# A transformer layer's MLP: from half batch by half batch with plain products to layer by layer with Strassen's seven products

## The chip, the cores and the metric

One NeuronCore of one Trainium2 chip. The metric is the device time of one execution in microseconds (us), the median of three runs. Engines: PE (TensorE), DVE (VectorE), ACT (ScalarE), POOL (GpSimd), SP (SyncE, which issues most loads and stores), and 16 DMA engines that move the data.

## The reference, cut to what matters

```python
# B, T, C = 8, 512, 512; x: (8, 512, 512); hidden sizes 1024, 1024, 512
h = _layernorm(x, axis=-1) * (1 + ca) + sa
x = x + ga * _L0_attn_ref(h, L0_attn_W_attn, L0_attn_W_proj)
h = _layernorm(x, axis=-1) * (1 + cb) + sb
# _L0_ffn_ref:
x1 = relu(einsum('bpd,hd->bph', h,  W1) + b1)   # 512 -> 1024
x2 = relu(einsum('bpd,hd->bph', x1, W2) + b2)   # 1024 -> 1024
out = einsum('bpd,od->bpo', x2, W3) + b3        # 1024 -> 512
x = x + gb * out
```

ca, sa, ga, cb, sb, gb are modulation vectors per batch. Everything is f32.

## The kernel before, in words

Each f32 product is made of three matmuls. An operand is split into a high part (its value rounded to fp32r) and a low part (the rest), and the high-high, low-high and high-low products are summed in PSUM (`TERMS`). So each operand costs a cast, mostly on ACT, and a subtraction, mostly on DVE.

The program has two parts. `attention` (the first 45% of the time) computes everything up to the attention output per batch and leaves it in DRAM as `attn_dram`. It isn't touched. `mlp` then does the rest. The diff replaces it whole.

`mlp` before works on half a batch (256 tokens, `CH`) at a time, sixteen in all, in a loop over the batches, with the first and last written out. All weights are loaded and split once at the start (`strips_hi` L1086 on ACT, `strips_lo` L1180 on DVE) and stay in SBUF. For a half batch PE does, in this order (`chunk` in the tensor block):

- layer 1 (`hidden`, L1268): 8 blocks of 128 features, 4 x 3 matmuls each, weights stationary, 256 tokens moving;
- turning the attention rows of the next half batch (L1230);
- layer 2 (L1268): 8 blocks of 8 x 3 matmuls, and after two of them the projection of the next half batch (`project`, L1249, 24 matmuls of 512 columns);
- turning the normalised rows of the next half batch (L1239);
- layer 3 (`last_layer`, L1249): 2 blocks of 128 tokens, 8 x 3 matmuls each, data stationary, 512 output columns moving.

ACT applies bias and ReLU to each block of features (L1080) and modulates the turned rows (L1072). DVE casts and subtracts to get the two parts (L1132, L1134), adds the gated attention output to the residual, takes the row statistics and normalises (L1142 to L1158), and finishes the output (L1170 to L1174). POOL only raises the variance to the power -0.5 (L1047). Activations never leave SBUF. The residual `res_tiles` is loaded from x, changed in place and stored from there. The order on every engine is written out by hand, and semaphores count what is done. An engine takes its instructions strictly in that order.

## Time and profile before

| what | us |
|---|---|
| median of three runs (1613.67 to 1619.86) | 1615.04 |
| the profiled execution | 1619.41 |
| its span, first to last instruction | 1617.6 |
| PE busy | 1540.7 (95%) |
| DVE busy | 938.1 (58%) |
| ACT busy | 637.5 (39%) |
| POOL busy | 441.5 (27%) |

The span is what the trace covers. The execution's own time has 1.8 us around it. Line numbers (L1268) are those of the kernel before. Matmuls overlap, so the time that one takes from start to end (0.283 us for 256 columns) is more than the distance from one to the next.

### The profile page before, as it was taken

What the parts mean: (1) busy time and instruction counts of PE and PEld (TensorE: products, weight loads), DVE (VectorE), ACT (ScalarE), POOL (GpSimd) and SP (SyncE); (2) the same over time, 40 slices, a digit from 0 to 9 for tenths busy, and PEclk for the clock granted to TensorE, in tenths of its full rate; (3) what the DMA queues carried; (4) which work ended last, traced back from release to release, by engine and by line L of the source; (5) the groups of instructions that cost most, each with busy time, mean ns of one, the idle gap of its engine ahead of it and who ended that gap; (6) DMA issues with size and microseconds to landing.
All of it is one profiled execution on the core that took longest, in us unless ns stands there. A gap on an engine that the chain in (4) does not pass through costs nothing.

```text
span 1617.6 us, 31407 instructions
## 1 busy us (share of the span) xinstructions
PE 1540.7 (95%) x12112; PEld 1369.6 (85%) x12112; DVE 938.1 (58%) x2199; ACT 637.5 (39%) x1280; POOL 441.5 (27%) x459
## 2 busy tenths in 40 slices
PE   7899999999999999966899999999999999999998
PEld 6678788878888878855899999999999999999998
DVE  4477877787778777646644444444544444444442
ACT  2166666666666666654312121212121212121221
POOL 2156666666666666660000000000000000000000
PEclk9799999999999999987999999999999999999999
DMA  6534343434343433316201001110111011100100
GB/s 215 151 80 126 87 125 87 126 86 126 87 119 93 119 93 93 93 30 223 94 34 47 27 20 48 46 30 31 34 47 46 2 47 46 40 21 34 46 14 14
DMA packets 80546, 118.33 MB, mean 73 GB/s; under 512 B 10632, under 2 KB 31112, under 8 KB 80400
## 3 DMA queue, kind: packets, MB, share of 16 engines
q1 hardware_dynamic: 72416, 105.19, 24.1%
q10 hardware_dynamic: 7984, 11.03, 1.9%
q8 instruction: 111, 1.82, 0.5%
q14 instruction: 35, 0.29, 0.1%
HBM read 48.52 MB, written 16.81 MB: 40 GB/s over the span
## 4 chain that ended last, share of the span: by engine, by line
PE 52%; DVE 1%; DMA 1%; issue 0%; SPq 0%; ACT 0%; POOL 0%; DVEq 0%; POOLq 0%
PE feature L1268 34%; PE token L1249 17%; PE feature L1239 1%; PE token L1230 1%; DVE w L1180 1%; DMA b_rows<-b 0%; DMA w_ring<-wproj_t 0%; DVE y L1134 0%; SPq L1010 0%; DVE y L1132 0%; ACT w L1086 0%; DVE attn_tiles L1158 0%; POOL mlp_rstd L1047 0%; DVE gated L1170 0%; DVE res_tiles L1145 0%
## 5 line engine op out<-in xcount | busy, mean ns | idle before, releaser
L1268 PE MATMUL feature<-y,w 128*128 128x256 f32 x3072 | 376.2, 283 | 6.5 <-DVE w L1180 6.5
L1268 PEld LDWEIGHTS feature<-y,w 128*128 128x128 f32 x3072 | 372.9, 189 | 8.0 <-DVE w L1180 6.7
L1080 ACT ACTIVATE mlp_full<-feature,b_cols 128x256 f32<-128x256 f32 x256 | 120.1, 474 | 649.5 <-PE feature L1268 561.2
L433 POOL TENSOR_TENSOR prob_lo<-prob,prob_hi 128x512 f16<-128x512 f32 x256 | 297.1, 1165 | 143.4 <-ACT prob L537 142.9
L1132 DVE CAST y<-mlp_full 128x256 fp32r<-128x256 f32 x256 | 75.0, 293 | 304.1 <-ACT mlp_full L1080 303.7
L530 ACT ACTIVATE prob_hi<-key_score 128x512 f16<-128x512 f32 x320 | 191.0, 597 | 134.7 <-PE key_score L828 132.3
L1047 POOL TENSOR_TENSOR mlp_rstd<-mlp_var_eps,mlp_minus_half 128x2 f32<-128x2 f32 x16 | 11.1, 696 | 802.9 <-DVE mlp_var_eps L1153 802.9
L739 PE MATMUL lin<-h_parts,wqkv 128*128 128x512 f32 x768 | 219.5, 410 | 1.1 <-DVE h_parts L582 1.1
L1268 PEld LDWEIGHTS feature<-turned,w 128*128 128x128 f32 x1536 | 188.2, 190 | 8.2 <-DVE w L1180 3.8
L1268 PE MATMUL feature<-turned,w 128*128 128x256 f32 x1536 | 189.4, 283 | 5.8 <-DVE turned L1134 3.4
L537 ACT ACTIVATE prob<-key_score 128x512 f32<-128x512 f32 x320 | 190.5, 595 | 0.0
L701 DVE TENSOR_REDUCE row_max<-score 128x1 f32<-128x512 f32 (+2 forms) x384 | 180.4, 498 | 13.8 <-PE score L815 13.1
L1249 PE MATMUL token<-w,y 128*128 128x512 f32 x768 | 183.5, 398 | 0.0
L1249 PEld LDWEIGHTS token<-w,y 128*128 128x128 f32 x768 | 143.4, 188 | 33.7
L739 PEld LDWEIGHTS lin<-h_parts,wqkv 128*128 128x128 f32 x768 | 144.0, 196 | 30.0 <-DVE h_parts L582 2.5
L815 PE MATMUL score<-stack 96*128 96x512 f32 (+3 forms) x512 | 156.2, 367 | 0.0
L828 PE MATMUL key_score<-stack 98*128 98x512 f32 (+3 forms) x512 | 144.7, 345 | 0.0
L848 PEld LDWEIGHTS o_bank<-v_parts,prob_hi 128*128 128x128 f16 x1280 | 100.1, 99 | 28.9 <-issue 25.5
L848 PE MATMUL o_bank<-v_parts,prob_hi 128*128 128x97 bf16 x1280 | 117.3, 212 | 5.2 <-POOL prob_lo L433 2.5
L848 PE MATMUL o_bank<-v_parts,prob_lo 128*128 128x65 bf16 x1280 | 114.4, 196 | 0.0
L1134 DVE TENSOR_TENSOR y<-mlp_full,y 128x256 fp32r<-128x256 f32 x256 | 108.9, 425 | 8.7
L749 PE MATMUL lin<-wqkv,h_parts 128*128 128x256 f32 x768 | 108.9, 284 | 0.0
(93 smaller groups left out, 1927.6 us busy)
## 6 DMA issues: line engine op xcount, KB each, us to landing
stack<-qk_parts SPq DMA_DIRECT2D x384, 128.0 KB, 2.4
x_tiles<-x SPq DMA_DIRECT2D x32, 256.0 KB, 3.8
attn_dram<-o_rows SPq DMA_DIRECT2D x32, 256.0 KB, 2.3
attn_tiles<-attn_dram SPq DMA_DIRECT2D x16, 512.0 KB, 5.0
res_tiles<-x SPq DMA_DIRECT2D x16, 512.0 KB, 3.5
out<-res_tiles ACTq DMA_DIRECT2D x16, 512.0 KB, 3.0
w_ring<-w_t SPq DMA_DIRECT2D x12, 512.0 KB, 5.6
wmod_sb<-wmod SPq DMA_DIRECT2D x4, 1024.0 KB, 6.3
```

Of the source, the lines that this page charges most:

```text
L433: nc.gpsimd.tensor_tensor(prob_lo[:, key[1] % 2, u, :], prob[:, u, :], prob_hi[:, key[1] % 2, u, :], ALU.subtract).then_inc(lo_pool, 1)
L530: nc.scalar.activation(prob_hi[:, q % 2, u, :], bank[:], ACT.Exp, scale=SOFTMAX_SCALE, bias=P_SHIFT)
L537: nc.scalar.activation(prob[:, u, :], bank[:], ACT.Exp, scale=SOFTMAX_SCALE, bias=P_SHIFT)\
L701: last = nc.vector.reduce_max(row_max[:, p % 2, hh, t:t + 1], bank[:, col:col + P * (t + 1)], AX.X)
L739: mm = nc.tensor.matmul(lin_bank_of((QK, f))[:], wqkv[:, wl, c, at:at + P], h[:, hl, c, :], start=(c == 0 and k == 0), stop=(c == NC_ - 1 ...
L749: mm = nc.tensor.matmul(lin_bank_of((V, g, t))[:, 0:C // 2], h[:, hl, c, t * P:(t + 1) * P], wqkv[:, wl, c, at:at + C // 2], start=(c == 0 ...
L815: mm = nc.tensor.matmul(bank[:, col:col + n], rows[:, 0, t * P:(t + 1) * P], rows[:, 1, 0:n], start=False, stop=True, skip_group_check=True)
L828: mm = nc.tensor.matmul(bank[:, col:col + n], rows[:, 1, t * P:(t + 1) * P], rows[:, 0, t * P:T], start=False, stop=True, skip_group_check ...
L848: mm = nc.tensor.matmul(o_bank[:, i * VW + low:(i + 1) * VW], part[:, p % 2, u, at:at + P], v[:, j, head, low:VW], start=(j == 0 and part ...
L1080: nc.scalar.activation(full[:, f % 2, :], fbank[f % 4][:, 0:CH], ACT.Relu, bias=bias[:, f:f + 1])\
L1249: mm = nc.tensor.matmul(bank[:], data[:, dl, c, t * P:(t + 1) * P], weights[:, wl, c, :], start=(c == 0 and i == 0), stop=(c == chunks - 1 ...
L1268: mm = nc.tensor.matmul(fbank[f % 4][:, 0:CH], weights[:, wl, c, f * P:(f + 1) * P], data[:, dl, c, :], start=(c == 0 and i == 0), stop=(c ...
```

## The change

The MLP now runs layer by layer over all batches: layer 1 for batches 0 to 7 (`EXPAND`), then layer 2 (`MIDDLE`), then layer 3 (`CONTRACT`), 24 chunks of one batch each, without a loop. Each chunk is the product of a weight matrix and a data matrix, both cut in 2 x 2 blocks, by Winograd's form of Strassen's scheme. Seven half-size products `product(n, s)`, s = 0 to 6, take the place of eight. Each still is three matmuls per term, now all with 256 columns.

- The sums of data blocks that four of the operands need are made by POOL (`sums`, 4 per chunk), those of the weights by POOL and DVE, once per layer (`w1_sums`, `w2_sum`, `w3_sums`).
- Operand s of chunk n is cast by ACT (`hi`) and subtracted by DVE (`lo`) into a ring of three buffers. Its buffer is free when product s - 3 is done.
- The seven results go to three pairs of PSUM banks (`SUMS`). ACT copies the first (`first_product`), DVE adds the others up to the four result blocks (`second_sum`, `third_sum`, `make_c22`, `make_c21`, `make_c12`), and C11 is accumulated by PE.
- ACT applies bias and ReLU in place (`relu`, 16 instructions a chunk), and SP stores the four blocks to `y_dram` (64 stores of 512 KB). Two layers load them back block by block (`load_block`, 64 loads).
- The residual after attention, with b3 times the gate already added by POOL, goes to `x2_dram` and is loaded again in the last layer, where DVE multiplies the blocks by the gate (`gate`) and POOL adds them (`add_gated`).
- Only weights of the layer at work are in SBUF. The middle layer's are loaded and split during the chunks 5 to 8, the last layer's in chunk 15.
- Projection, turning, statistics and normalising of the following batches are hung into the products of the first layer by the table `AUX_AT`: (s, m) gives the place, the number behind the kind says how many batches ahead. They share two PSUM banks.

```diff
-CH = 256
-CT = CH // P
-HALVES = T // CH
...
+HB = T // 2
+EXPAND, MIDDLE, CONTRACT = range(3)
+CHUNKS = 3 * B
+STEPS = 7
+K_TILES, M_TILES, BANKS = (2, 4, 4), (4, 4, 2), (2, 2, 1)
...
+SUMS = ("a", "b", "e", "a", "b", "e", "b")
+FRESH = (True, True, True, False, True, True, False)
...
+AUX_AT = {(0, 3): [(PROJ, 1, 2)], (1, 3): [(PROJ, 1, 3)],
+          (2, 1): [(TURNED, 2, 0)], (2, 3): [(TURNED, 2, 1)], (3, 1): [(TURNED, 2, 2)], (3, 3): [(TURNED, 2, 3)],
+          (5, 1): [(ROWS, 1, 0)], (5, 3): [(ROWS, 1, 1)], (6, 1): [(ROWS, 1, 2)],
+          (6, 3): [(ROWS, 1, 3), (PROJ, 2, 0), (PROJ, 2, 1)]}
...
+            def load_block(n, i):
+
+                if n > B:
+                    m = n - 1
+                    if i < 2:
+                        sp.wait_ge(op_sum, sum_no(m, 3) + 1)
+                        sp.wait_ge(op_ready, op_no(m, 0) + 1)
+                    elif i == 2:
+                        sp.wait_ge(op_ready, op_no(m, 3) + 1)
+                    else:
+                        sp.wait_ge(op_ready, op_no(m, 6 if layer(m) < CONTRACT else 5) + 1)
+                elif i >= 2:
+                    sp.wait_ge(op_sum, sum_no(B - 1, 3) + 1)
+                    sp.wait_ge(op_ready, op_no(B - 1, 6) + 1)
+                sp.wait_ge(y_out[i], 16 * (n - B + 1))
+                sp.dma_start(blk[i][:], y_view(n - B, i).rearrange("p (c n) -> p c n", n=HB)).then_inc(blk_in[i], 16)
+
+            def store_block(n, i):
+                sp.wait_ge(relu_done, relu_no(n, i, 3) + 1)
...
+            def load_x2(k):
+                if k >= 2:
+                    for half in range(2):
+                        sp.wait_ge(out_done[half], 16 * (k - 1))
+                sp.wait_ge(x2_out[k % 2], 16 * (k // 2 + 1))
+                sp.dma_start(x2t[:, k % 2], rows_of(x2_dram, k)).then_inc(x2_in[k % 2], 16)
+
...
+            def contract(n):
+                k = n - CONTRACT * B
+                if k:
+                    store_out(k - 1, 0)
+                else:
+                    store_block(n - 1, C12)
+                if k and k + 1 < B:
+                    load_gate(k + 1)
+                if k + 1 < B:
+                    load_block(n + 1, 0)
+                    load_block(n + 1, 1)
+                if k and k + 1 < B:
+                    load_x2(k + 1)
+                if k + 1 < B:
+                    load_block(n + 1, 2)
+                    load_block(n + 1, 3)
+                store_out(k, 1)
+
...
+            def sums(n):
...
+                block_wait(pool, n, 1)
+                block_wait(pool, n, 3 if contract_op else 0)
+                if n:
+                    pool.wait_ge(op_ready, op_no(n - 1, 4) + 1)
+                if contract_op:
+                    nc.gpsimd.tensor_tensor(t1, b[1], b[3], ALU.add).then_inc(op_sum, 1)
+                else:
+                    nc.gpsimd.tensor_tensor(t1, b[1], b[0], ALU.subtract).then_inc(op_sum, 1)
+
+                block_wait(pool, n, 0 if contract_op else 3)
+                ring_wait(pool, n, 1)
+                pool.wait_ge(op_sum, sum_no(n, 0) + 1)
+                if contract_op:
+                    nc.gpsimd.tensor_tensor(low[0], t1, b[0], ALU.subtract).then_inc(op_sum, 1)
+                else:
+                    nc.gpsimd.tensor_tensor(low[0], b[3], t1, ALU.subtract).then_inc(op_sum, 1)
+
+                block_wait(pool, n, 2)
+                if n:
+                    last = max(s for s, i in TEMP_OPS[layer(n - 1)].items() if i == 1)
+                    pool.wait_ge(op_ready, op_no(n - 1, last) + 1)
+                pool.wait_ge(op_sum, sum_no(n, 1) + 1)
+                if contract_op:
+                    nc.gpsimd.tensor_tensor(t4, b[2], low[0], ALU.subtract).then_inc(op_sum, 1)
+                else:
+                    nc.gpsimd.tensor_tensor(t4, low[0], b[2], ALU.subtract).then_inc(op_sum, 1)
+
+                ring_wait(pool, n, 2)
+                if contract_op:
+                    nc.gpsimd.tensor_tensor(low[1], b[0], b[1], ALU.subtract).then_inc(op_sum, 1)
+                else:
+                    nc.gpsimd.tensor_tensor(low[1], b[3], b[1], ALU.subtract).then_inc(op_sum, 1)
+
...
+            def modulate(k, c):
+                no = AUX_NO[(ROWS, k, c)]
+                act.wait_ge(aux_done, no + 1)
+                if k:
+                    act.wait_ge(op_sum, sum_no(k - 1, 3) + 1)
+                    act.wait_ge(op_ready, op_no(k - 1, 0 if c < 2 else 6) + 1)
+                nc.scalar.activation(h2[:, c, :], aux_bank[no % 2][:], ACT.Identity,
+                                     scale=mod_cols[:, 1, NC_ + c, k:k + 1], bias=mod_cols[:, 1, c, k:k + 1])\
+                    .then_inc(rows_act, 1)
...
+            def relu(n, i):
+                bias = (b1_cols, b2_cols)[layer(n)]
+                for m in range(4):
+                    here = made[i][:, m // 2, m % 2 * HB:m % 2 * HB + HB]
+                    src = here
+                    if i == C11:
+                        if m % 2 == 0:
+                            act.wait_ge(prod_done, done_no(n, 3, m // 2) + 1)
+                        if m == 0 and n:
+                            act.wait_ge(y_out[C11], 16 * n)
+                        src = acc["a"][m // 2][:, m % 2 * HB:m % 2 * HB + HB]
+                    elif m % 2 == 0:
+                        act.wait_ge(post_done, post_no(n, {C22: Y22, C21: Y21, C12: Y12}[i], m // 2) + 1)
+                    f = 4 * BLOCKS[i][0] + m
+                    nc.scalar.activation(here, src, ACT.Relu, bias=bias[:, f:f + 1]).then_inc(relu_done, 1)
...
+            def expand(n):
+                k = n
+                last = k == B - 1
+                hi(n, 2)
+                if n:
+                    relu(n - 1, C12)
+                first_product(n)
+                hi(n, 3)
+                hi(n, 4)
+                for c in (0, 1):
+                    if k + 2 < B:
+                        turned_hi(k + 2, c)
+                hi(n, 5)
+                for c in (2, 3):
+                    if k + 2 < B:
+                        turned_hi(k + 2, c)
+                if last:
+                    w2_hi(0)
+                relu(n, C11)
+                hi(n, 6)
+                for c in (0, 1):
+                    if k + 1 < B:
+                        modulate(k + 1, c)
+                if last:
+                    w2_hi(1)
+                relu(n, C22)
+                hi(n + 1, 0)
+                relu(n, C21)
+                for c in (2, 3):
+                    if k + 1 < B:
+                        modulate(k + 1, c)
+                hi(n + 1, 1)
+
+            def middle(n):
...
+            def second_sum(n):
+                for half in halves(n):
+                    dve.wait_ge(prod_done, done_no(n, 1, half) + 1)
+                    dve.wait_ge(p1_done, p1_no(n, half) + 1)
+                    if half == 0:
+                        buffer_free(n, C12)
+                    nc.vector.tensor_tensor(part(u2, n, half), bank_of(n, 1, half)[:], part(p1, n, half), ALU.add)\
+                        .then_inc(post_done, 1)
...
+            def middle(n):
+                make_c12(n - 1)
+                lo(n, 1)
+                lo(n, 2)
+                if n == B:
+                    w2_lo(4)
+                lo(n, 3)
+                second_sum(n)
+                if n == B:
+                    w2_lo(2)
+                lo(n, 4)
+                third_sum(n)
+                if n == B:
+                    w2_lo(3)
+                lo(n, 5)
+                if n == B:
+                    w2_lo(6)
+                lo(n, 6)
+                if n == B:
+                    w2_lo(5)
...
+            def product(n, s):
+                where, tiles = layer(n), K_TILES[layer(n)]
+                if n % B == 0:
+                    pe.wait_ge(w_ready, W_NO[(where, s, 1) if where == MIDDLE else (where, s)] + 1)
+                pe.wait_ge(op_ready, op_no(n, s) + 1)
+                data = op(n, s)
+                for m in range(M_TILES[where]):
+                    if m % 2 == 0:
+                        sum_free(n, s, m // 2)
+                    again = not FRESH[s] or m % 2 == 1
+                    dst = bank_of(n, s, m // 2)[:, m % 2 * HB:m % 2 * HB + HB]
+                    for c in range(tiles):
+                        for i, (wl, dl) in enumerate(TERMS):
+                            begin = FRESH[s] and m % 2 == 0 and c == 0 and i == 0
+                            end = c == tiles - 1 and i == 2
+                            cols = slice(m * P, (m + 1) * P)
+                            if where == CONTRACT:
+                                mm = nc.tensor.matmul(dst, data[:, dl, c, cols], w3[s][:, wl, c, :],
+                                                      start=begin, stop=end, skip_group_check=again)
+                            else:
+                                w = (w1, w2)[where][s]
+                                mm = nc.tensor.matmul(dst, w[:, wl, c, cols], data[:, dl, c, :], start=begin, stop=end,
+                                                      skip_group_check=again)
+                    if m % 2:
+                        mm.then_inc(prod_done, 1)
+                    if where == EXPAND:
+                        for item in aux_at(n, s, m):
+                            aux(item)
+
```

In full length it is 1,500 lines. The functions of the same name per engine (`expand`, `middle`, `contract`) set the order on each engine; the DMA stores and loads all stand in SP's queue.

Three places of the new order, on the engines that wait or are waited for there. The first is ACT, in a chunk before (one half batch; `mlp_full` is the result of bias and ReLU, `turned` the operand):

```order
L1113 DMA out<-res_tiles 128x2x512 [waits out_ready]
L1080 ACTIVATE mlp_full<-feature,b_cols 128x256 [waits f_split,f_done] x8
L1065 CAST turned<-token 128x256 [waits t_done] x4
L1080 ACTIVATE mlp_full<-feature,b_cols 128x256 [waits f_split,f_done] x8
L1072 ACTIVATE mlp_full<-feature,mlp_mod_now 128x256 [waits mlp_mod_ready,f_split,f_done]
L1072 ACTIVATE mlp_full<-feature,mlp_mod_now 128x256 [waits f_split,f_done] x3
L1113 DMA out<-res_tiles 128x2x512 [waits out_ready]
```

and in a chunk of the expanding layer now, from the modulation of the first two blocks of normalised rows to the cast of the next chunk's operands (`p_c` holds C22, `u_c` C21 and then C12, `h` the modulated rows, `op` an operand):

```order
L1438 ACTIVATE h<-aux,mod_cols 128x512 [waits op_ready,op_sum,aux_done] x2
L1482 ACTIVATE p_c<-p_c,b_cols 128x256 [waits post_done]
L1482 ACTIVATE p_c<-p_c,b_cols 128x256
L1482 ACTIVATE p_c<-p_c,b_cols 128x256 [waits post_done]
L1482 ACTIVATE p_c<-p_c,b_cols 128x256
L1448 CAST op<-h 128x512 [waits prod_done,rows_act]
L1482 ACTIVATE u_c<-u_c,b_cols 128x256 [waits post_done]
L1482 ACTIVATE u_c<-u_c,b_cols 128x256
L1482 ACTIVATE u_c<-u_c,b_cols 128x256 [waits post_done]
L1482 ACTIVATE u_c<-u_c,b_cols 128x256
L1438 ACTIVATE h<-aux,mod_cols 128x512 [waits op_ready,op_sum,aux_done] x2
L1456 CAST op<-op_whole 128x512 [waits op_sum] x2
```

The modulation of the last two blocks (L1438, second place) now stands behind the ReLUs of C22 and C21 and the cast of the next chunk's operand 0.

The second is DVE, at the split of the second layer's weights. Before, in the first half batch (`w` are weights, `y` the split data):

```order
L1132 CAST y<-mlp_full 128x256 [waits f_act]
L1134 TENSOR_TENSOR y<-mlp_full,y 128x256 [waits f_hi]
L1180 TENSOR_TENSOR w<-w_ring,w 128x1024 [waits mlp_w_hi]
L1132 CAST y<-mlp_full 128x256 [waits f_act]
L1134 TENSOR_TENSOR y<-mlp_full,y 128x256 [waits f_hi]
L1180 TENSOR_TENSOR w<-w_ring,w 128x1024 [waits mlp_w_hi]
L1180 TENSOR_TENSOR w<-w_ring,w 128x512 [waits mlp_w_hi] x8
```

and now, in the first chunk of the middle layer (L1751 splits weights, L1663 operands, L1680 and L1689 are `second_sum` and `third_sum`, with `sum_b` and `sum_e` PSUM banks):

```order
L1663 TENSOR_TENSOR op<-blk,op 128x1024 [waits op_hi]
L1680 TENSOR_TENSOR u_c<-sum_b,p_c 128x512 [waits y_out1,p1_done,prod_done]
L1680 TENSOR_TENSOR u_c<-sum_b,p_c 128x512 [waits p1_done,prod_done]
L1751 TENSOR_TENSOR w_2<-w_2_whole,w_2 128x1024 [waits mlp_w_hi] x2
L1663 TENSOR_TENSOR op<-op_sum,op 128x1024 [waits op_hi]
L1689 TENSOR_TENSOR u_c<-sum_e,u_c 128x512 [waits y_out2,post_done,prod_done]
L1689 TENSOR_TENSOR u_c<-sum_e,u_c 128x512 [waits post_done,prod_done]
L1751 TENSOR_TENSOR w_3<-w_3_whole,w_3 128x1024 [waits mlp_w_hi] x2
```

The splits were next to each other, ahead of layer 2. Now each stands behind a sum that waits for a product of the same chunk.

The third is SP. Before, the loads of one chunk in the loop:

```order
L998 DMA attn_tiles<-attn_dram 128x2x512
L58 ISA [waits out_done0]
L1001 DMA res_tiles<-x 128x2x512 [waits out_done0]
L58 ISA [waits out_done0]
L993 ISA [waits t_taken]
L993 DMA gate_attn<-gate_dram 128x512
L1035 ISA
L993 ISA [waits out_ready]
L993 DMA gate_mlp<-gate_dram 128x512
```

and now of a chunk of the contracting layer (`x_tiles` are the residual's, `blk` the four data blocks):

```order
L1235 DMA out<-x_tiles 128x2x512 [waits add_done] x2
L1223 DMA gate_mlp<-gate_dram 128x512 [waits g_done]
L1131 DMA blk<-y_dram 128x1024 [waits y_out0,op_ready,op_sum]
L1131 DMA blk<-y_dram 128x1024 [waits y_out1,op_ready,op_sum]
L1230 DMA x_tiles<-x_dram 128x4x512 [waits x2_out0,out_done1,out_done0]
L1131 DMA blk<-y_dram 128x1024 [waits y_out2,op_ready]
L1131 DMA blk<-y_dram 128x1024 [waits y_out3,op_ready]
L1235 DMA out<-x_tiles 128x2x512 [waits add_done] x2
```

The loads of blocks 2 and 3 for the next chunk stand behind the residual's load, which waits for both stores of the output before.

## Rows read from the trace of the kernel before

**Rows 1.** Page: the span, busy time by engine, the chain by line

```profile
span 1617.6 us, 31407 instructions
...
PE 1540.7 (95%) x12112; PEld 1369.6 (85%) x12112; DVE 938.1 (58%) x2199; ACT 637.5 (39%) x1280; POOL 441.5 (27%) x459
...
PE feature L1268 34%; PE token L1249 17%; PE feature L1239 1%; PE token L1230 1%; DVE w L1180 1%; DMA b_rows<-b 0%; DMA w_ring<-wproj_t 0%; DVE y L1134 0%; SPq L1010 0%; DVE y L1132 0%; ACT w L1086 0%; DVE attn_tiles L1158 0%; POOL mlp_rstd L1047 0%; DVE gated L1170 0%; DVE res_tiles L1145 0%
```

**Rows 2.** Stretches of five half batches: us, busy of each engine, PEclk, DMA share, GB/s

```profile
core 0: us, PE busy (x) PEld busy (x) DVE busy (x) ACT busy (x) POOL busy (x), PEclk, DMA share, GB/s
859.22:912.48 53.26, 53.26 (x377) 49.83 (x377) 25.19 (x62) 10.71 (x24) 0.70 (x1) 1.00 0.10 36
...
sum 267.42, PE 266.61 PEld 249.25 DVE 126.10 ACT 53.62 POOL 3.48; mean PE 53.32 PEld 49.85 DVE 25.22 ACT 10.72 POOL 0.70
```

**Rows 3.** Chain in order of time: start, duration, what

```profile
894.20 17.28 PE feature L1268 x144
912.48 11.23 PE token L1249 x48
...
1600.88 11.24 PE token L1249 x48
```

**Rows 4.** SP's queue in order of time, first load of the MLP

```profile
726.46 0.39 SPq L998 DMA_DIRECT2D attn_tiles<-attn_dram  x1
```

**Rows 5.** ACT by form, MLP; two ReLUs in a row; ACT by form, attention

```profile
L1080 ACT ACTIVATE mlp_full<-feature,b_cols 128x256 f32<-128x256 f32 x256 | 120.1, 474 | 649.5 <-PE feature L1268 561.2 <-issue 60.8 <-DVE res_tiles L1174 23.1
L1086 ACT CAST w<-w_ring 128x1024 fp32r<-128x1024 f32 x12 | 12.6, 1049 | 4.7 <-DMA w_ring<-w_t 4.6
...
926.63 0.91 ACT L1080 ACTIVATE mlp_full<-feature,b_cols 128x256 f32<-128x256 f32 x2 [11.75 <-PE feature L1268]
...
L537 ACT ACTIVATE prob<-key_score 128x512 f32<-128x512 f32 x314 | 186.9, 595 | 0.0
L472 ACT ACTIVATE full<-lin,mod_now 128x512 f32<-128x512 f32 x32 | 25.0, 781 | 18.0 <-PE lin L729 9.9 <-POOL h_parts L407 8.0
```

**Rows 6.** DVE by form, MLP

```profile
L1142 DVE TENSOR_TENSOR gated<-token,gate_attn 128x512 f32<-128x512 f32 x32 | 22.1, 691 | 32.3 <-PE token L1249 32.3
L1180 DVE TENSOR_TENSOR w<-w_ring,w 128x1024 fp32r<-128x1024 f32 x12 | 14.4, 1217 | 0.1
```

**Rows 7.** POOL by form, attention

```profile
L433 POOL TENSOR_TENSOR prob_lo<-prob,prob_hi 128x512 f16<-128x512 f32 x251 | 291.3, 1165 | 141.6 <-ACT prob L537 141.3
L407 POOL TENSOR_TENSOR h_parts<-full,h_parts 128x512 fp32r<-128x512 f32 x32 | 40.6, 1278 | 30.3 <-DVE h_parts L582 30.3
L444 POOL TENSOR_TENSOR o_rows<-o_sum,o_rcp 128x256 f32<-128x256 f32 x61 | 37.5, 615 | 0.0
```

**Rows 8.** Loads and stores of the MLP; stretches with full queues

```profile
attn_tiles<-attn_dram SPq DMA_DIRECT2D x16, 512.0 KB, 5.0
out<-res_tiles ACTq DMA_DIRECT2D x16, 512.0 KB, 3.0
...
730.00:735.00 5.00, 1.97 (x8) 1.57 (x8) 2.24 (x4) 2.70 (x6) 0.00 (x0) 0.50 0.95 324
735.00:740.00 5.00, 4.03 (x10) 3.19 (x11) 1.82 (x5) 2.95 (x6) 0.00 (x0) 0.50 0.99 389
```

**Rows 9.** Stretches around PE's wait for the second layer's weights

```profile
765.00:770.00 5.00, 2.94 (x26) 2.70 (x24) 4.90 (x10) 3.16 (x5) 0.00 (x0) 1.00 0.83 256
770.00:775.00 5.00, 0.60 (x3) 0.60 (x4) 4.93 (x9) 4.06 (x6) 0.00 (x0) 0.59 0.94 303
775.00:780.00 5.00, 5.00 (x33) 5.00 (x33) 3.77 (x6) 2.60 (x5) 0.00 (x0) 0.73 0.79 260
```

**Rows 10.** DVE by form, attention, two tensors of SBUF

```profile
L707 DVE TENSOR_TENSOR prob_lo<-prob,prob_hi 128x512 f16<-128x512 f32 x63 | 46.3, 735 | 22.3 <-ACT prob L537 22.3
L617 DVE TENSOR_TENSOR wqkv<-wqkv_raw,wqkv 128x1024 fp32r<-128x1024 f32 x6 | 8.3, 1407 | 0.7 <-ACT wqkv L506 0.6
```

More of the change, by code:

```diff
@@ new lines, in ring_wait, with temp_view, bank_of, halves @@
+    def ring_wait(engine, n, s):
+        if op_no(n, s) >= 3:
+            before = divmod(op_no(n, s) - 3, STEPS)
+            engine.wait_ge(prod_done, done_no(*before, BANKS[layer(before[0])] - 1) + 1)
+    def temp_view(n, i):
+        return temp[i][:, 0:K_TILES[layer(n)], :]
+    def bank_of(n, s, half):
+        return acc[SUMS[s]][half if layer(n) < CONTRACT else n % 2]
+    def halves(n):
+        return range(BANKS[layer(n)])
+    def part(tile, n, half):
+        return tile[:, half if layer(n) < CONTRACT else n % 2, :]
@@ new lines, in _, with aux_free, turn_attention @@
+            for k in range(B):
+                expand(k)
+            for k in range(B):
+                middle(B + k)
+            for k in range(B):
+                contract(2 * B + k)
+            make_c12(CHUNKS - 1)
+            gate(CHUNKS - 1, C12)
+        @whole.tensor
+        def _(pe):
+            def aux_free(item):
+                no = AUX_NO[item]
+                if no < 2:
+                    return
+                kind, k, i = AUX[no - 2]
+                taken = {TURNED: att_lo, PROJ: proj_taken, ROWS: rows_act}[kind]
+                pe.wait_ge(taken, 4 * k + i + 1)
+            def turn_attention(k, c):
+                bank = aux_bank[AUX_NO[(TURNED, k, c)] % 2]
@@ L1234, in turn_rows @@
             def turn_rows(k, c):
+                bank = aux_bank[AUX_NO[(ROWS, k, c)] % 2]
                 if c == 0:
[L1236 to L1251 removed]
@@ L1307 @@
+            for item in AUX_FIRST:
+                aux(item)
+            for n in range(CHUNKS):
+                for s in range(STEPS):
+                    product(n, s)
 def kernel(L0_attn_x, L0_attn_W_attn, L0_attn_W_proj, L0_ffn_W1, L0_ffn_b1, L0_ffn_W2, L0_ffn_b2, L0_ffn_W3,
```

1048 lines of the change are left out of this document (723 added, 325 removed).

## The prediction

> **What bounds the kernel now.** The page comes first. TensorE (PE) is busy 95% of the span, and two lines of the MLP alone, L1268 and L1249, hold half of the chain that ended last [rows 1]. The table of stretches then says whether that is a steady bound: over five consecutive half batches PE is busy 266.61 of 267.42 us at a granted clock of 1.00 (2.4 GHz), while DVE needs 126.10, ACT 53.62 and POOL 3.48 [rows 2]. So a half batch lasts 53.5 us, all of it PE, and every matmul taken away shortens it until something else arrives late. The chain prices a matmul better than its listed latency: 144 with 256 columns take 17.28 us, 0.120 each, and 48 with 512 columns 11.23 us, 0.234 each [rows 3].
>
> The MLP starts with the first load at 726.46 [rows 4] and ends with its last matmul at 1600.88 + 11.24 = 1612.1 [rows 3]: 885.7 us. Sixteen half batches are 855.7. The other 30 are the start: loads, weight splitting, PE at half clock.
>
> **Term 1, matmuls: -87.5 us.** Per batch the three layers are now 576 matmuls of 256 columns and 96 of 512: 69.1 + 22.5 = 91.6 us. Seven half-size products of 24, 48 and 24 matmuls are 672 of 256 columns: 80.6. That saves 10.9, times 8 is 87.5. The listing confirms 5,376. Projection and turns stay, 107.0 - 91.6 = 15.4 us a batch. Note that the third layer gains less than an eighth: 168 x 0.120 = 20.2 against 22.5, since 256 columns cost 0.120, more than half of 0.234.
>
> What is added lies on the other engines. Per batch in the middle layer: DVE 7 x 1.22 + 10 x 0.69 = 15.4 us [rows 6], ACT 7 x 1.05 + 2 x 0.6 + 16 x 0.47 = 16.1 [rows 5], POOL 4 x 2.27 = 9.1, all under 40.3 us of PE. POOL's 2.27 for 1,024 elements is the line through 0.615 for 256 and 1.165 for 512; the row that writes fp32r gives 1.278 for 512, so 2.5 is the upper bound. I take the first, since the new sums write plain f32 as the 256 row does [rows 7]. Going through DVE's and ACT's queue in the middle layer, every operand is ready more than 2 us before its product. I cost that layer at no wait.
>
> **Term 2, the start: -7.** Weights of the middle layer are no longer needed here, but attention rows, projection weights and x come in 1 MB pieces. By the rates of [rows 8], the projection weights land at about 734.5. Two casts of 1.05, four of 0.6 and the last split bring PE's first projection to 739.8; four of them, the first at half clock, end at 752.4; gating, add, statistics and normalising 756.8; four turns and modulations 761; operand 0 at 762.5; turning batch 1 through two banks 766.5; its two projections 772. PE has then done 23.1 us of work that counts in the steady sum, so 772 - 726.5 - 23.1 = about 23 is lost, where it was 30. Bounds -15 and +3.
>
> **Term 3, a wait in the expanding layer: +21.** A chunk is 20.2 + 15.4 = 35.6 us of PE. Its last item but one is projection of the batch after next, which takes the bank of the third turn and so waits until ACT has modulated it. In ACT's order that stands behind a long queue. From the end of the second turn of rows: modulate 0.78, four ReLUs 1.8 (two take 0.91), cast 0.6 [rows 5], DVE's split of operand 0 0.69, first half of C21 0.69 [rows 6], four ReLUs 1.8, modulate 0.78, hand-overs 0.3: 7.4 us. PE meanwhile has one product, 2.9, and two turns, 1.0. That leaves 3.5 us, in the six chunks that have such a projection: 21. If ReLUs ran at the pace of plain casts it were 14; with a DVE slowed as below, and a hand-over more, 33.
>
> **Term 4, expanding to middle layer: +20.** Now the 1,024 x 1,024 weights' sums and splits stand among DVE's work. In chunk 6 two pairs of sums (2.3 each) go before C22 and C21; through ACT's ReLUs, the modulation and two POOL sums, product 1 of chunk 7 is ready 6.8 us late. Chunk 7 has 20.2 us of PE and about as much of DVE, so nothing is regained: middle products 0 and 1 are 0.3 and 1.2 late. Then the splits of weights 2 and 3 each stand behind the DVE sum that waits for the product just ended: 1.3 + 2.3 = 3.6 us [rows 6] before the next can start, 1.7 more for weight 2, whose DVE queue is late already, and 2.6 for weight 5. 6.8 + 0.3 + 1.2 + 5.3 + 3.6 + 2.6 = 20. Bounds 12 and 30: with sums and splits 16% quicker or slower and one wait less or more.
>
> **Term 5, contracting layer: +40.** PE needs 20.2 us a chunk. There is a loop that needs more. Call A the moment POOL has added the last gated block. SP then stores the half output; behind it in SP's queue stand the gate, blocks 0 and 1, the residual's load (which waits until that store has landed, 3.0 [rows 8], so A + 3.4), and only then blocks 2 and 3. Gate, residual and four blocks are 3.4 MB; at 370 GB/s, between the two full stretches of 324 and 389 [rows 8], 9.2 us, from A + 3.3 to A + 12.5. POOL's first sum needs block 3. Four sums of 2.27 and four adds of 1.165 later [rows 7] comes the next A: 12.5 + 9.1 + 4.7 = 26.3 us. The bound is then no engine but this loop. The change of layer delays the first loads (C12's ReLU behind weight casts), so POOL's second sum ends 23.2 us into chunk 16, the next at 49.4, five periods later 180.7; two sums, cast, split and five products: 202 against 161.3. That is 40. With 2.5 us a sum and 14 us of loads it is 57; with blocks landing at A + 10 it is 25.
>
> The Trainium skill, DMA: Bandwidth & Descriptors (Where 436 GB/s comes from), says that between HBM and SBUF the HBM side binds at about 358 GB/s a core. This trace disagrees, with 389 in a stretch [rows 8]. By the page's figure the loop would be 0.3 us longer, 2 us in all (an estimate from that page).
>
> **Term 6, clock: +4.** After a gap of some 6 us the granted clock was 0.59 in the next stretch and 0.73 in that after, then 1.00 again [rows 9]: about 3.3 us at 1.2 GHz, 1.6 lost. Term 4 has two or three such gaps. In the contracting layer PE has 5 us to spare. Gaps of 3.5 us I take as free (bound: 1.6 each, 10).
>
> **Sum.** -87.5 - 7 + 21 + 20 + 40 + 4 = -9.5. The tail (sum, gate, add, store) stays as long. Against the profiled execution, 1619.4 us (span 1617.6), that gives 1609.9; this execution lay 4.4 above the median of the runs shown, 1615.0, so 1605.5. All low bounds together give -52, all high ones +49.
>
> **Rivals.**
> *The loads keep up.* If blocks 2 and 3 land before POOL needs them, the contracting layer is held only by POOL's three sums, cast and split, 9.2 us where PE's three products give 8.6. Term 5 falls from 40 to about 8: 1573.5. For it: the 512 KB loads of the MLP landed in 5.0 us in the median, and 3.0 for stores [rows 8], with DMA mostly idle. Against it: SP's order, in which the loads are not issued earlier whatever they take.
>
> *POOL slows beside DVE: slower than before.* Place: POOL's sums and adds in the loop of term 5. Beside a busy POOL, DVE's two-input subtraction from SBUF took 0.735 and 1.407 us where the same shapes take 0.69 and 1.22 in the MLP [rows 6, 10]. POOL's rows were all taken in the attention part, where DVE reads mostly PSUM; now DVE's seven splits a chunk read two tensors of SBUF. Six sums' worth of POOL work lies in each of six periods, 40 in all with the last. To be 0.5% slower than before needs 17.5 us more, 0.44 a sum: it decides from 2.71 us. At 2.85 (23 us), and DVE 16% slower in terms 3 and 4 (4), +27: 1632.5. Beside this stands the Trainium skill, GPSIMD Engine Reference (8. Key points): POOL shares its SBUF interfaces with DVE, with contention when DVE has two SBUF inputs. By that rule the trace agrees for DVE; for POOL no row shows it.
>
> *The clock falls at each gap of the expanding layer.* +10: 1615.5, no change. For it: [rows 9]. Against: the stretch in which that gap began still shows 1.00.
>
> *The change does not do what it says:* the listing excludes it.
>
> **How the numbers follow.** Forecast 0.5, loads keep up 0.15, POOL slows 0.25, clock 0.1. A run can tell 0.5%, 8 us, from no change. The forecast's own spread is about 20 us around 1605.5: 0.3 faster, 0.1 same, 0.1 slower. The first rival is faster, the second slower but for 0.05, the third mostly same. Faster 0.49, same 0.2, slower 0.31. The range, 1570 to 1642, takes in both rivals and leaves out 2 in 10: an unseen wait above, the low bounds together below.
>
> **What would show it.** Middle chunks of 40.3 us with PE busy throughout; L1990 and L1994 at 0.120 a matmul (right for term 1). PE's L1934 waiting for ACT's L1438 six times, 3.5 each (term 3). PE waiting for DVE's weight splits L1751 near the first middle chunk (term 4). Contracting chunks at 26 us, POOL's L1310 waiting for the block's load, sums of 2.27 (term 5). Contracting chunks of 21 would prove the first rival, sums over 2.7 the second. I am wrong altogether if the middle layer waits too.

## The result, and the profile after

The changed kernel takes 1682.6 us (median of 4 runs, 1680.8 to 1687.1), the kernel before 1615.4 beside it: a ratio of 1.042, 95% interval 1.0385 to 1.0447. That is slower by 4%, and outside the range of the prediction. The profiled execution spans 1679.0.

The page, with the lines that answer to [rows 1]:

```profile
span 1679.0 us, 30398 instructions
...
PE 1479.9 (88%) x12112; PEld 1340.3 (80%) x12112; DVE 1056.3 (63%) x1795; ACT 789.9 (47%) x1430; POOL 830.2 (49%) x661
...
PE 21%; POOL 5%; DMA 5%; DVE 2%; issue 2%; ACT 1%; SPq 0%; POOLq 0%; DVEq 0%; ACTq 0%
```

PE is busy for 61 us less and its share of the span falls from 95% to 88%. (The matmuls taken away are 87.5 us; the difference is mostly matmuls that took longer, as told below. The chain in the last line is followed over little more than a third of the span.) What a steady stretch looks like now, in the middle layer and in the contracting one (windows, as in [rows 2]):

```profile
1140.00:1380.00 240.00, 240.00 (x2002) 240.00 (x2001) 100.84 (x101) 89.15 (x150) 55.84 (x25) 1.00 0.30 109
...
1500.00:1530.00 30.00, 20.74 (x159) 20.53 (x159) 17.55 (x16) 7.72 (x8) 15.42 (x8) 0.84 0.43 150
1530.00:1560.00 30.00, 20.61 (x163) 20.41 (x162) 17.72 (x16) 7.72 (x8) 15.64 (x9) 0.84 0.44 149
```

The middle layer is PE alone. In the contracting layer no engine is busy for more than 70% of the time, and PE waits. The waits of PE over the MLP:

```profile
PE sum_b L1990 <- DVE op L1663: 69.2, 8, 10.3
PE aux L1934 <- ACT h L1438: 18.3, 6, 3.1
PE aux L1944 <- DVE norm_tiles L1651: 14.4, 1, 14.4
...
PE sum_b L1994 <- DVE op L1663: 7.3, 1, 7.3
...
PE sum_b L1994 <- issue: 5.3, 1, 5.3
PE sum_e L1994 <- DVE w L1751: 5.0, 2, 3.1
PE sum_a L1994 <- DVE w L1751: 3.1, 1, 3.1
```

From the timeline of PE and SP the MLP, first load to last matmul, divides as below (us). The last column is the number that the prediction implies.

| stretch | after | predicted |
|---|---|---|
| first load to product 0 of chunk 0 | 60.2 | 46 |
| chunks 0 to 5 (expanding) | 240.8 | 235 |
| chunks 6 to 8 | 119.3 | 112 |
| chunks 9 to 15 (middle) | 284.3 | 282 |
| chunks 16 to 23 (contracting) | 247.8 | 201 |
| sum | 952.4 | 876 |

Before, it was 885.7. So 67 us were lost there, 76 more than forecast; the attention part was 5.9 us shorter in this execution (first load at 720.55 against [rows 4]), which has nothing to do with the change: in the kernels below, which leave it alone too, that load stands between 722 and 726.

PE's time in each stretch can be split into its waits (every idle time of more than 0.1 us) and the rest, and the rest compared with the same matmuls at their steady pace (an expanding chunk without a wait takes 34.8 us in the kernels below, not 35.6):

| stretch | waits of PE | the rest | the rest at the steady pace |
|---|---|---|---|
| chunks 0 to 5 | 20.0 | 220.8 | 209 |
| chunks 6 to 8 | 22.7 | 96.6 | 88 |
| chunks 9 to 15 | 1.8 | 282.5 | 282.2 |
| chunks 16 to 23 | 70.1 | 177.7 | 161.3 |

The slower matmuls stand behind the waits, and the granted clock shows why. First the 5 us behind a wait of 3.05 us in the expanding layer, then chunks 0 to 5 together:

```profile
815.00:820.00 5.00, 4.98 (x12) 3.93 (x13) 0.00 (x0) 1.55 (x3) 3.79 (x3) 0.50 0.26 105
785.00:1021.00 236.00, 217.23 (x1462) 201.23 (x1463) 138.03 (x230) 98.35 (x195) 116.13 (x85) 0.94 0.43 151
```

**The loop of the contracting layer**, in the timeline of SP and of POOL, for one period. SP:

```profile
1564.06 1.64 SPq L1235 DMA_DIRECT2D out<-x_tiles  x2
1565.74 0.50 SPq L1223 DMA_DIRECT2D gate_mlp<-gate_dram  x1
1566.35 1.35 SPq L1131 DMA_DIRECT2D blk<-y_dram  x2
1568.52 0.37 SPq L1230 DMA_DIRECT2D x_tiles<-x_dram  x1
1568.98 1.27 SPq L1131 DMA_DIRECT2D blk<-y_dram  x2
```

POOL:

```profile
1561.76 3.53 POOL L1385 TENSOR_TENSOR x_tiles<-x_tiles,u_c 128x512 f32<-128x512 f32 x2
1579.88 2.34 POOL L1310 TENSOR_TENSOR op_sum<-blk 128x1024 f32<-128x1024 f32 x1 [14.59 <-DMA blk<-y_dram]
...
1589.49 2.26 POOL L1385 TENSOR_TENSOR x_tiles<-x_tiles,c 128x512 f32<-128x512 f32 x1
1591.71 2.26 POOL L1385 TENSOR_TENSOR x_tiles<-x_tiles,p_c 128x512 f32<-128x512 f32 x1
1593.93 2.25 POOL L1385 TENSOR_TENSOR x_tiles<-x_tiles,u_c 128x512 f32<-128x512 f32 x1
```

The last add ends at 1565.3. The residual's load is issued 3.2 us later, as forecast, and the last two blocks behind it. The first sum starts 14.6 us after that add (forecast 12.5), when block 3 has landed, four sums take 9.6 with their hand-overs (9.1), and four adds about 8 (4.7): 32.2 instead of 26.3. The adds are the surprise: 2.26 us each where [rows 7] gave 1.165. And DVE's lines say the same of the splits:

```profile
L1663 DVE TENSOR_TENSOR op<-op_whole,op 128x1024 fp32r<-128x1024 f32 x8 | 22.2, 2770 | 30.9 <-POOL op_sum L1328 30.7
L1663 DVE TENSOR_TENSOR op<-blk,op 128x1024 fp32r<-128x1024 f32 x10 | 16.5, 1653 | 1.8 <-ACT op L1448 1.8
...
L1689 DVE TENSOR_TENSOR u_c<-sum_e,u_c 128x512 f32<-128x512 f32 x4 | 2.8, 688 | 1.1 <-PE sum_e L1990 1.1
```

Operations that read two SBUF tensors are up to 2.3 times as long as in [rows 6]; those with one input from PSUM are as short as there. POOL's sums keep their 2.34 us here, since DVE waits for them (30.7 us, in the first of these lines).

### The profile page after: what moved, and what is told of

The parts are those of the page before. It is cut to its first block and busy times, and to the rows that moved or that the text cites. A ratio compares the mean times of both kernels' runs of the same rounds, so it can differ in the third digit from the quotient of the medians.

```text
span 1679.0 us, 30398 instructions
## 1 busy us (share of the span) xinstructions
PE 1479.9 (88%) x12112; PEld 1340.3 (80%) x12112; DVE 1056.3 (63%) x1795; ACT 789.9 (47%) x1430; POOL 830.2 (49%) x661
## 5 line engine op out<-in xcount | busy, mean ns | idle before, releaser
L1994 PE MATMUL sum_b<-op,w 128*128 128x256 f32 x1728 | 221.8, 287 | 14.5 <-DVE op L1663 7.3
L1994 PEld LDWEIGHTS sum_b<-op,w 128*128 128x128 f32 x1728 | 215.2, 195 | 15.5 <-DVE op L1663 7.5
L1994 PE MATMUL sum_e<-op,w 128*128 128x256 f32 x1152 | 148.2, 286 | 5.0 <-DVE w L1751 5.0
L1994 PE MATMUL sum_a<-op,w 128*128 128x256 f32 x1152 | 147.1, 286 | 5.1 <-DVE w L1751 3.1
L1990 PE MATMUL sum_b<-w,op 128*128 128x256 f32 x576 | 87.7, 318 | 69.2 <-DVE op L1663 69.2
L1994 PEld LDWEIGHTS sum_e<-op,w 128*128 128x128 f32 x1152 | 143.1, 194 | 6.0 <-DVE w L1751 5.4
L1994 PEld LDWEIGHTS sum_a<-op,w 128*128 128x128 f32 x1152 | 142.6, 194 | 6.5 <-DVE w L1751 3.3
L1990 PEld LDWEIGHTS sum_b<-w,op 128*128 128x128 f32 x576 | 84.5, 227 | 70.8 <-DVE op L1663 62.9
L1934 PE MATMUL aux<-wproj,turned 128*128 128x512 f32 x384 | 106.4, 437 | 22.9 <-ACT h L1438 18.3
L1663 DVE TENSOR_TENSOR op<-op_whole,op 128x1024 fp32r<-128x1024 f32 (+1 forms) x48 | 90.7, 1893 | 51.9 <-POOL op_sum L1328 42.9
L844 PEld LDWEIGHTS o_bank<-v_parts,prob_hi 128*128 128x128 f16 x1280 | 98.6, 98 | 29.5 <-issue 25.7
L1663 DVE TENSOR_TENSOR op<-blk,op 128x1024 fp32r<-128x1024 f32 x48 | 70.3, 1465 | 76.8 <-ACT op L1448 76.8
```

The costliest lines, as they stand in the source:

```text
L844: mm = nc.tensor.matmul(o_bank[:, i * VW + low:(i + 1) * VW], part[:, p % 2, u, at:at + P], v[:, j, head, low:VW], start=(j == 0 and part ...
L1663: nc.vector.tensor_tensor(op(n, s)[:, 1], whole_value, f32(op(n, s)[:, 0]), ALU.subtract)\
L1934: mm = nc.tensor.matmul(bank[:], turned[:, dl, c, t * P:(t + 1) * P], wproj[:, wl, c, :], start=(c == 0 and i == 0), stop=(c == NC_ - 1 an ...
L1990: mm = nc.tensor.matmul(dst, data[:, dl, c, cols], w3[s][:, wl, c, :], start=begin, stop=end, skip_group_check=again)
L1994: mm = nc.tensor.matmul(dst, w[:, wl, c, cols], data[:, dl, c, :], start=begin, stop=end, skip_group_check=again)
```

## The experiments

Two theories. **The loop:** SP's order and POOL's queue set the period. **Exclusion:** DVE with its inputs in SBUF and POOL hold each other up so far that they all but take turns, and their times add up.

**The price by itself.** A kernel of DVE, POOL and ACT operations alone, and no matmul.

> This kernel computes nothing of the block: it only prices operations. It runs DVE forms alone (12 each: subtraction of two SBUF tensors with 1,024 elements, PSUM plus SBUF with 512, tensor_scalar with 512 from SBUF, copy of 1,024), POOL's tensor_tensor alone (1,024 and 512), and then each DVE form while POOL runs its sum, and ACT's copy beside POOL. Theory A (DVE and POOL hold each other up, the rest of the kernel has no part in it): alone 1.22, 0.69, 0.54 on DVE and about 2.3 and 1.2 on POOL; beside POOL's 1,024-element sum the two-input form and tensor_scalar take 2.2 to 2.5 each, as long as POOL's, the form from PSUM stays near 0.7, ACT's copy near 1.05; POOL's 1,024 stays within 0.2 of its time alone, its 512 goes from 1.2 to 2.2. Theory B (DMA traffic into SBUF slows them): with no DMA here every form beside POOL is within 10% of its time alone.

Its groups of instructions (names beginning with d_two_by, d_scalar_by and d_copy_by are DVE's beside POOL, those with d_dve alone):

```profile
L91 POOL TENSOR_TENSOR p_two_by<-c_in,d_in 128x1024 f32<-128x1024 f32 x8 | 26.2, 3309 | 0.2 <-POOLq L94 0.2
L89 POOL TENSOR_TENSOR p_two_by<-c_in,d_in 128x512 f32<-128x512 f32 x12 | 25.5, 2156 | 3.1 <-DVEq L71 3.1
...
L91 POOL TENSOR_TENSOR p_scalar_by<-c_in,d_in 128x1024 f32<-128x1024 f32 x8 | 19.9, 2524 | 0.2 <-POOLq L94 0.2
...
L91 POOL TENSOR_TENSOR p_psum_by<-c_in,d_in 128x1024 f32<-128x1024 f32 x8 | 18.4, 2342 | 4.6 <-DVEq L71 4.6
L91 POOL TENSOR_TENSOR p_pool<-c_in,d_in 128x1024 f32<-128x1024 f32 x8 | 18.4, 2338 | 47.7 <-DVEq L71 47.7
L89 POOL TENSOR_TENSOR p_pool<-c_in,d_in 128x512 f32<-128x512 f32 x12 | 14.7, 1260 | 0.2 <-DVEq L71 0.2
L60 DVE TENSOR_TENSOR d_dve_two<-a_in,b_in 128x1024 f32<-128x1024 f32 x12 | 13.7, 1216 | 0.0
...
L62 DVE TENSOR_TENSOR d_psum_by<-bank,a_in 128x512 f32<-128x512 f32 x12 | 7.3, 679 | 0.2 <-DVEq L71 0.2
L65 DVE TENSOR_SCALAR d_dve_scalar<-a_in,stat 128x512 f32<-128x512 f32 x12 | 5.6, 538 | 0.2 <-POOLq L94 0.2
```

Alone DVE's subtraction takes 1.22 and POOL's sum 2.34. Together each takes about 3.3: eight of each need 26.2 us, where 8 x (1.22 + 2.34) is 28.5. Twelve POOL sums of half the size beside it need 25.5 instead of 14.7. So POOL slows too, which was expected only for its small operation. The tensor_scalar goes from 0.54 to 2.56, the copy of 1,024 elements from 0.68 to 2.82, both about one operation of POOL's. The form from PSUM stays at 0.68 and leaves POOL at 2.34; ACT's copy stays at 1.04. No DMA runs here, so DMA is not the cause. Theory A is right in kind and too low in size for the two-input form (2.2 to 2.5 expected, 3.35 measured).

**The contracting layer, in three steps.** First SP's order:

```
-store_out(k - 1, 0)
-load_gate(k + 1)
 load_block(n + 1, 0)
 load_block(n + 1, 1)
-load_x2(k + 1)
 load_block(n + 1, 2)
+store_out(k - 1, 1)
+store_out(k - 1, 0)
 load_block(n + 1, 3)
-store_out(k, 1)
+load_gate(k + 1)
+load_x2(k + 1)
```

> SP's order in the contracting layer only: blocks 0, 1 and 2 of the next chunk before the stores of the last, then block 3, gate and residual. Theory A (the loop is set by SP's order and by loads landing 14.5 us after POOL's last add): block 3 lands 7 us after that add, so the period of a chunk goes from 31.8 to 23 to 25 us, times 7 is -48 to -60 us, near 1627. Theory B (the contention of DVE and POOL is what holds the layer, the loads are covered by it): the period stays above 29, less than -20 us.

Second the adds, from POOL's `contract` to DVE's `gate`; and then both edits:

```
-                add_gated(n)
...
                 nc.vector.tensor_tensor(dst, src, rows, ALU.mult).then_inc(g_done, 1)
...
+                nc.vector.tensor_tensor(done, done, dst, ALU.add).then_inc(add_done, 1)
```

> The four adds of the residual move from POOL to DVE, each right behind its gate. Theory A (the loop runs through POOL's queue: blocks, four sums, four adds): POOL's 8 us of adds leave it, and the loop now closes over two chunks (loads behind the store of chunk k-1, products of chunk k+1), so that the period is 22 to 24 us: -55 to -65 us. Theory B (DVE, slowed beside POOL, becomes the bound): seven splits of which four at 2.3, three PSUM sums, four gates and four adds are 22 to 26 us a chunk: -40 to -55. Theory C (the landing of the loads alone sets it): less than -20.

> Both edits, SP's order and the adds on DVE. Theory A (SP's order and POOL's adds are the loop): nothing but PE is left, period 20.2 to 21.5, -70 to -80 us, about 1607. Theory B (DVE beside POOL is a bound of its own behind the loop): period 23 to 25, no more than 5 us better than the better of the two edits alone.

Third the sums as well, from POOL to DVE's `contract`, with SP's new order, and again with SP's order as the change has it:

```
-                    sums(n + 1)
...
+                dve_sum(n, 3)
                 make_c12(n - 1)
...
-                lo(n, 1)
...
                 lo(n + 1, 0)
+                for i in range(3):
+                    dve_sum(n + 1, i)
                 make_c21(n)
+                lo(n + 1, 1)
                 gate(n, C21)
```

> Both edits of the last kernel, and DVE instead of POOL makes the four sums of each contracting chunk but the first, so that POOL does nothing there. Theory A (DVE and POOL exclude each other while DVE reads two SBUF tensors, so that their times add up): DVE now has 7 x 1.22 + 4 x 1.22 + 5 x 0.69 + 8 x 0.69 = 22.4 us a chunk and no partner, the period falls from 27.3 to 23 to 24.5: -20 to -28 us against both edits together, near 1640. Theory B (an engine's load is what its rows say, POOL and DVE run side by side): DVE gets 4.9 us more a chunk beside its 26, the period rises: +15 us or more.

> Adds and sums of the contracting layer on DVE, with SP's order as the change has it (stores, gate, blocks 0 and 1, residual, blocks 2 and 3). Theory A (SP's order makes block 3 land some 14 us after the last add, wherever the sums are made): DVE's first sum then waits for the load in each chunk, period about 27 instead of 23.5: +20 to +28 us against the kernel with the new order, near 1660. Theory B (with POOL out of the loop the order of the loads has no part): within 5 us of it.

| kernel | median us | contracting layer |
|---|---|---|
| the change | 1682.6 | 247.8 |
| SP's order | 1662.4 | 225.4 |
| adds on DVE | 1668.0 | 233.4 |
| both | 1664.1 | 229.5 |
| both, sums on DVE | 1636.1 | 205.0 |
| adds and sums on DVE, old SP order | 1641.8 | 203.3 |

SP's order gives 20.2 us, far less than the loop promised (48 to 60). Its rival said under 20 and a period above 29; behind the first chunk the periods are 26.6 to 28.4, so neither theory is met, and the rival is the nearer. The adds on DVE give 14.6, which only the third theory (the landing of the loads sets it) allowed. Both edits together give no more than one, as theory B had it, though at periods of 27.8 to 29.5 us and not its 23 to 25. With the new order alone DVE is busy 86% of the time, its splits and gates two to three times as long:

```profile
1500.00:1530.00 30.00, 24.54 (x191) 24.13 (x190) 25.91 (x18) 8.34 (x10) 19.23 (x9) 0.94 0.52 168
...
L1662 DVE TENSOR_TENSOR op<-blk,op 128x1024 fp32r<-128x1024 f32 x13 | 31.2, 2400 | 1.5 <-ACT op L1447 1.5
L1772 DVE TENSOR_TENSOR u_c<-u_c,gate_mlp 128x512 f32<-128x512 f32 x9 | 19.4, 2156 | 0.3
```

With both edits POOL has only its sums left, and they wait for a block in every chunk:

```profile
1538.95 2.40 POOL L1309 TENSOR_TENSOR op_sum<-blk 128x1024 f32<-128x1024 f32 x1 [18.16 <-DMA blk<-y_dram]
```

That block's load is issued when DVE has split the chunk's operand 5 (1535.2), lands 3.7 us later, and the four sums end at 1550.2: 11.3 us, where four alone are 9.4. So a loop through load, sums and splits was still there, with DVE's and POOL's longer operations in it.

Then 4.9 us of work a chunk more on DVE, and none on POOL, made it 28 us faster. With all on DVE, windows and groups:

```profile
1500.00:1530.00 30.00, 27.17 (x224) 26.76 (x224) 27.09 (x32) 9.72 (x10) 0.00 (x0) 1.00 0.59 193
...
L1660 DVE TENSOR_TENSOR op<-blk,op 128x1024 fp32r<-128x1024 f32 x15 | 18.3, 1220 | 2.2 <-ACT op L1445 2.2
...
L1770 DVE TENSOR_TENSOR u_c<-u_c,gate_mlp 128x512 f32<-128x512 f32 x10 | 6.9, 688 | 0.2
```

Every operation of DVE is back at its time alone, and theory B, by which the period had to rise, is refuted. How much of the 28 us is exclusion is not settled by it: the same edit also takes four POOL operations (9.4 us alone, 11.3 as they ran) out of the loop and puts 4.9 us of DVE in their place. No run here has POOL's slower sums without the contention.

The period is 23.5 us at its best (product 2 starts at 1517.82 and 1541.32), where DVE's rows sum to 22.4; the other periods behind the first are 24.8 to 26.2. PE's waits are the same in all of them, 0.3 and 2.51 us. What differs is product 2 behind the wait of 2.51, here where the clock held and where it fell:

```profile
1517.82 3.13 PE L2021 MATMUL sum_e<-w,op 128*128 128x256 f32 x24 [2.51 <-DVE op L1660]
1564.82 5.49 PE L2021 MATMUL sum_e<-w,op 128*128 128x256 f32 x24 [2.51 <-DVE op L1660]
```

It took 3.13 us twice and 4.4 to 5.5 in the other five.

The last row of the table was a miss for the loop: with the sums off POOL, SP's old order costs the layer nothing that shows (203.3 us against 205.0; the whole kernel is 5.8 us slower in the median, and of the 3.7 by which the profiled executions differ 2.9 lie in the attention part). DVE idles there before its first sum, which needs block 3 (5.8 us in four chunks), but the last add comes early in a chunk, and the landing 14 to 15 us later falls beside other DVE work. So SP's order was a bound only while POOL's sums and adds stood in one queue, slowed by DVE. Behind it stood a second bound, 27 to 29 us, with the slowed operations of both engines in it.

**The expanding layer.** ACT's order:

```
 hi(n + 1, 0)
-relu(n, C21)
 for c in (2, 3):
     modulate(k + 1, c)
+relu(n, C21)
```

> In ACT's order of an expanding chunk the modulations of turns 2 and 3 stand ahead of the ReLUs of block C21 (nothing else is changed). Theory A (the projection of the batch after next waits for a bank that ACT has not read): the six waits of 3.05 us go, -18, and with them the stretch at a lower clock behind each, up to -8: -18 to -26 us. Theory B (the wait only moves to product 0 or 1 of the next chunk, whose operands are as late): less than -8.

1656.9, so -25.8. All six waits of 3.05 us are gone; chunks 0 to 5 take 210.5 instead of 240.8. Of these 30.3 us, 18.3 are waits, so 12, or 2 a gap, came from the clock behind it: it stands at 1.00 now where it was 0.94.

```profile
785.00:1000.00 215.00, 213.61 (x1521) 200.24 (x1520) 151.53 (x238) 100.59 (x200) 119.78 (x87) 1.00 0.48 171
```

**The first middle chunk.** `w2_hi` and `w2_lo` of products 2, 3, 6 and 5 stand one place earlier; on DVE, for the first two:

```
     w2_lo(4)
+    w2_lo(2)
 lo(n, 3)
+    w2_lo(3)
 second_sum(n)
-    w2_lo(2)
 lo(n, 4)
 third_sum(n)
-    w2_lo(3)
```

> In the first middle chunk the weight splits of products 2, 3, 6 and 5 stand one place earlier on ACT and DVE, ahead of the DVE sum that waits for the product just ended. Theory A (each of those splits was late behind that sum): the waits of 3.05, 3.05 and 1.98 us go, -6 to -9 us. Theory B (DVE is short of time there in any case): -3 or less.

1675.0, -7.7: of the waits for L1751 one of 0.7 us is left, and chunks 6 to 8 take 107.9 instead of 119.3. Two larger waits stay as they were: 7.3 us before product 1 of chunk 7, and 5.6 before product 1 of chunk 8.

**The start.** POOL's `w1_sums` is split in two, the second half waiting for `x_norm`:

```
+w1_sums_first()
 for t in range(NT):
     add_rows(0, t)
 inverse_deviation(0)
-w1_sums()
+w1_sums_last()
```

In the change DVE and POOL stood so:

```profile
753.23 10.00 DVE L1651 TENSOR_SCALAR norm_tiles<-res_tiles,mlp_mean_var,mlp_rstd 128x512 f32<-128x512 f32 x4 [1.13 <-POOL mlp_rstd L1282]
...
753.16 2.34 POOL L1341 TENSOR_TENSOR w_whole<-c,u_c 128x1024 f32<-128x1024 f32 x1
```

> At the start of the MLP POOL makes the first two weight sums before it adds the residual of batch 0, and the last two only after DVE has normalised that batch. Theory A (DVE's normalising, 10.0 us for four, was held by POOL's sums): it takes 0.54 each again, the first product starts 6 to 9 us earlier: -6 to -9 us. Theory B (the start waits for loads or weight splits instead): -2 or less.

The normalising takes 0.54 us each again, and product 0 comes 49.9 us behind the first load instead of 60.2. That is 10.3 us, more than the 6 to 9 expected, but the run gained only 4.2, which is neither theory's number. PE's wait in chunk 0 for the gated rows grew from 1.73 to 4.90, and in the profile the contracting layer took 252.5, 4.7 more. In the four kernels that have the layer unchanged it took 247.8 to 252.5; their waits are 70.1 to 72.0 and the rest 177.7 to 180.5, so the scatter lies in both, and its cause is open.

**All together,** and on top of it one pair of weight sums moved, from chunk 6 to 7:

```
-if k == B - 2:
-    w2_sum(1)
...
 if last:
+    w2_sum(1)
     w2_sum(2)
```

> All edits so far in one kernel: SP's order, adds and sums on DVE in the contracting layer, modulations first, weight splits one place earlier, weight sums around the normalising. Theory A (the causes lie in different places and add up): 1636 - 26 - 8 - 4 = 1598 us, 1.2% faster than the kernel before the change. Theory B (a chunk that starts earlier only waits for loads or for DVE elsewhere): above 1608.

> The same, and DVE makes the second pair of sums of the middle layer's weights in chunk 7, after the split of operand 2, where it stood between the split of operand 0 and the sum for C21 of chunk 6. Theory A (that pair, 3.45 us beside POOL, and what it delays hold product 1 of chunk 7 back, which waits 5.5 to 7.3 us): -3 to -5 us against the kernel without it. Theory B (product 1 waits for POOL's sums of the operand alone, or the pair is late where it now stands): within 1 us, or slower.

1586.1 us, 0.982 of the kernel before (0.9795 to 0.9845), the fastest here: faster by 1.8% (whether it is a full 2% the interval leaves open) where the change was slower by 4.2%. It is 12 better than the sum; its contracting layer is 197.4, 8 less than with the DVE sums alone, which the sum does not hold. Of these 8, 6 are matmul time (171.3 instead of 177.3) and not waits (26.0 instead of 27.6). Moving the pair on top changed nothing: 1587.2, 1 us apart, as theory B said.

## Why the prediction was wrong

The forecast was 1605.5 us and the change took 1682.6. By stretches the 76 us that the MLP took more than forecast are 14 at the start, 6 in chunks 0 to 5, 7 in chunks 6 to 8, 2 in the middle layer and 47 in the contracting layer. The step that failed is the sum "12.5 + 9.1 + 4.7 = 26.3" of term 5: the loop was the right mechanism, and it takes 32.2. Two more terms were mis-sized, the start and the clock.

- **Term 1, -87.5: right.** A middle chunk is 40.32 us, a product of 48 matmuls 5.76, with no wait in 240 us. L1990's products are 2.88 apart.
- **Term 2, the start, -7: wrong by 14.** The step "gating, add, statistics and normalising 756.8" failed: four normalisings took 10.0 us, not 2.2, beside POOL's weight sums, and the clock was at 0.50 in the stretches after. The order was right, the price of a pair of operations wasn't. The experiment on the start gave 10.3 of the 14 back.
- **Term 3, +21: the wait was right** in place, number and size (six of 3.05 instead of 3.5).
- **Term 4, +20: near.** PE waited 22.7 us in chunks 6 to 8. Product 1 of chunk 7 waited 7.34 where 6.8 was said, and the splits of weights 2, 3 and 5 cost 3.05, 3.05 and 1.98, somewhat less than said. Wrong was product 1 of chunk 8, taken as 1.2 late: it waited 5.28 (the row with `issue`), with POOL's sum for it waiting for a block that landed 3 us after the chunk began. The two errors cancel in part, which is luck.
- **Term 5, +40: it was 86.** The loop was there, in the order described. Its six periods up to POOL's second sum for the last chunk took 193.5 us, where 157.5 was forecast; the first of those sums came 6.1 us later than said and the last products took 3.7 more. Mis-sized were the four adds (8 us instead of 4.7: 2.26 for 1.165 each), then the landing (14.6 for 12.5) and the sums (9.6 for 9.1). Nothing was said of a second bound behind the loop.
- **Term 6, +4: too small, and for a wrong reason.** "Gaps of 3.5 us I take as free" failed: 12 us came back when the six gaps went. The rival "clock falls at each gap" was right for that layer, its 10 us nearly so. Chunks 6 to 8 lost another 9 us in this way, and in the contracting layer the matmuls took 16 us longer than at full clock; there they were not costed, since PE was said to have 5 us to spare. How much of those 16 lengthened the layer no run separates. Product 1 took up to 5.49 us there instead of 3.04.
- **The rival "POOL slows beside DVE"** had the mechanism and the wrong place. It was priced at the sums, with 2.71 us as the point from which it decides; in the change they took 2.34, since DVE was waiting for them. What slowed was the adds, and DVE itself. Taken over both, the six sums' worth of POOL work in a period took 17.6 us, 2.9 each, so its size for the loop was about right; its total of 1632.5 lacked the start and the clock. [rows 10] had been read as 7 and 16%. They are averages over operations of which few met POOL. The single ones in the trace of before show the contention in full (lines below this list: shortest, median and longest in ns). The rule cited from the Trainium skill, GPSIMD Engine Reference (8. Key points), was right, and the traces agree for both engines: 1.22 to 3.3 for DVE's subtraction, 2.34 to 3.3 for POOL's sum.
- **"The loads keep up"** was wrong for the change. It came nearly true once nothing of the layer was left on POOL, but a chunk then still took 23.5 us and more, not 21.

```profile
L707 DVE TENSOR_TENSOR prob_lo<-prob,prob_hi x64: 669/692/1757, 90.8 to 715.0; 128x512 f16<-128x512 f32 x64
...
L617 DVE TENSOR_TENSOR wqkv<-wqkv_raw,wqkv x6: 1210/1225/2346, 14.2 to 32.9; 128x1024 fp32r<-128x1024 f32 x6
```

Of the 64 operations of the first line three had a subtraction of POOL (L433) beginning beside them, and took 1.74 to 1.76 us; the other 61 took 0.67 to 0.74. Of the six of the second line one had POOL's L407 beside it and took 2.35, where the others took 1.21 to 1.23. The price was on record before the change, in the single operations and not in their mean.
